# Attention and mixture of experts on one core: the order of work in the expert stage, the loads of its records and the copies of its hidden layer changed

## The chip, the cores and the metric

One core of one Trainium2 chip runs the whole program. The metric is the device time of one execution in microseconds. Everything is computed in 32-bit floating point. TensorE multiplies matrices and writes to PSUM, VectorE and ScalarE do elementwise work and read PSUM back, GpSimd adds and scales rows and issues the indirect DMAs, and SyncE issues the plain DMAs.

## The reference, cut to what matters

```python
x = conv_attention(x)                    # local attention, 2 images of 32 x 32 tokens, 128 channels
t = tokens(x)                            # 2048 tokens of 128
t = t + additive_attention(norm(t))      # h = tanh(q_i + k_j + bh), e = h @ Wa
h = norm(t)
logits = h @ gate_w + gate_b             # 8 experts
idx = argmax(softmax(logits)); prb = max(softmax(logits))
pos = place of the token among those of its expert      # kept if pos < 320
hmid = relu(buf @ w1 + b1)               # buf: 8 experts x 320 slots x 128, w1: 128 x 512
y = (hmid @ w2 + b2) * prb               # w2: 512 x 128
t = t + nan_to_num(y, nan=0, posinf=1e4, neginf=-1e4)
```

## The kernel before

The work stands in one program for each engine, written out by hand; the engines meet at semaphores only, and each engine does its instructions in the order of its program. There are three stages: local attention, additive attention over 16 blocks of 128 query tokens (`p` counts them), and the experts. The change concerns the passage from the second to the third, and the third.

**From attention to records.** For each block p, `soften_main(p)` (ScalarE) takes the exponential of the energies, `turn_main(p)` (TensorE) transposes it in two halves of four blocks, `turned_main(p)` (VectorE) copies the halves to SBUF, `attend(p, half)` (TensorE) multiplies each with the tokens, and `attended(p)` and `normed(p)` (VectorE) make the record's contents. Then `turn_normed`, `logits` (TensorE) and `route(p)` (VectorE) pick the expert, `counts(p)` (TensorE) counts the tokens of each expert so far, `slotted(p)` (VectorE) turns that into the row of the record, and `scatter(p)` (GpSimd) writes the 128 records of the block to `xbuf` in DRAM. Of the last two blocks, the steps of p = 14 that follow `attend` are written among those of p = 15, behind the last energies.

A record is a row of 272 numbers: the normed token (C = 128), the token itself (128), the logits less their maximum (8) and the token's number, with 7 unused. `xbuf` has 2560 such rows, 20 tiles of 128. Experts take 320 rows each, so two experts share five tiles: `tiles_of(e)` gives an even expert the first two and an odd one the last three, the middle tile of the five being half of one and half of the other.

**Experts.** SyncE loads `xbuf` back in four DMAs of five tiles (`xe`, semaphores `ld_xe[q]`). TensorE turns five tiles at a time (`turn_slots(q)`) into banks 4 and 5, ScalarE copies them to `xeT` (`turned_slots`), `first_product(e)` multiplies with w1 into banks 0 to 3 (four matmuls of 320 columns, each shown as two instructions), `rectified(e)` adds the bias, takes the maximum with 0 and writes `h`: ScalarE for two of the four banks, VectorE for the other two. `second_product(e)` multiplies with w2 into slots of banks 6 and 7 (`slot_bank`), three parts for each expert, of 128, 128 and 64 rows. TensorE's order is: first product of e + 1, then second product of e.

VectorE ends the work in `slots_out(e)`: for each tile the product times `prb` plus the weighted bias row `b2w`, then over the two or three tiles of the expert together six operations that replace infinities and NaNs and add the token (`high`, `low`, `good`, `fill`, `fill`, `ye`). A helper `Chain` (`link`) puts a semaphore wait behind every operation. `weights(q)` (exponential on ScalarE, sum and reciprocal on VectorE) gives `prb` for five tiles. VectorE does it in the turn of expert 2q - 2 and says so with `prb_ready`. GpSimd scales the 20 bias rows and after that sends the 20 tiles to `out`:

```python
for q in range(NE // 2):
    pool.wait_ge(prb_ready, q + 1)
    for k in range(q * n, (q + 1) * n):
        last = nc.gpsimd.tensor_scalar(b2w[:, k, :], b2w[:, k, :], prb[:, k:k + 1], 1.0, ALU.mult, ALU.mult)
    last.then_inc(b2w_ready, 1)
```

Each send is an indirect DMA of 128 rows of 512 B, to the rows named by `dest`. The program ends when all have landed.

## Time and profile before

| | |
|---|---|
| median of 3 runs | 765.26 us (763.8 to 765.88) |
| the profiled execution | 758.97 us |
| its span in the trace | 757.2 us |
| busy: TensorE, VectorE, ScalarE, GpSimd | 532.6, 565.6, 579.9, 418.0 us |
| first issue of the loads of the records | at 687.79 us of the span |
| TensorE's last matmul ends | at 740.28 us |

The span runs from the first to the last event of the trace, and the execution's time lies 1.8 us above it. Busy time is an average over stages with different limits: the stage of the experts, from 692 us on, is a small part of it and has to be read by itself. An idle engine is shown with what ended its idle time.

### The profile page before, as it was taken

Reading aid. Unit: us, or ns where it says so; the run is one execution under the profiler, and the core shown is the slowest. Engines: PE = TensorE matmul, PEld = TensorE weight load, DVE = VectorE, ACT = ScalarE, POOL = GpSimd, SP = SyncE. Lnnn points to the kernel's source line nnn. Section 1 sums busy time; section 2 is a strip of 40 time slices with the busy share of each in tenths; the row PEclk is TensorE's granted clock in tenths of the full one; section 3 lists DMA queues with packets and bytes.
Section 4 is the critical chain, followed back from the end, with each engine's and each line's share of the span. In section 5 each row is a group of like instructions: output and inputs, shape, how many; then the busy total and the mean of one; then the engine's idle time right before and its main releaser. Section 6 shows DMA issues by size and latency. Waiting matters only on the chain.

```text
span 757.2 us, 11927 instructions
## 1 busy us (share of the span) xinstructions
PE 532.6 (70%) x4440; PEld 261.0 (34%) x4440; DVE 565.6 (75%) x1326; ACT 579.9 (77%) x385; POOL 418.0 (55%) x453
## 2 busy tenths in 40 slices
PE   7899998886357676675775786766666666744991
PEld 3666665662012131221221231221221221233870
DVE  3566688877986878878878788878878878741783
ACT  2367776655379999999999999999999999911210
POOL 2000000005448888888878878878878878601156
PEclk9899999998689999999999999999999999985996
DMA  9500000007000000000000000000000000004001
GB/s 324 164 3 1 2 2 2 2 1 292 0 1 0 5 12 1 12 8 4 12 1 12 12 0 13 12 1 13 12 0 12 12 1 12 10 6 149 2 11 39
DMA packets 11225, 22.22 MB, mean 29 GB/s; under 512 B 1232, under 2 KB 8434, under 8 KB 10400
## 3 DMA queue, kind: packets, MB, share of 16 engines
q1 hardware_dynamic: 9760, 18.56, 6.9%
q0 software_dynamic: 1408, 2.91, 1.1%
q8 instruction: 35, 0.57, 0.3%
q14 instruction: 22, 0.18, 0.1%
HBM read 14.73 MB, written 7.37 MB: 29 GB/s over the span
## 4 chain that ended last, share of the span: by engine, by line
issue 34%; ACT 30%; PE 16%; DVE 12%; POOL 2%; DMA 1%; POOLq 0%; DVEq 0%; ACTq 0%; SPq 0%
ACT arena L788 28%; PE ps L461 3%; PE ps L474 2%; PE ps L443 2%; POOL out L406 2%; DVE arena L1020 2%; DVE arena L871 2%; ACT pm L792 1%; PE ps L500 1%; PE ps L695 1%; PE ps L587 1%; PE ps L492 1%; PE ps L708 1%; PE ps L484 1%; DVE mean L918 1%
## 5 line engine op out<-in xcount | busy, mean ns | idle before, releaser
L370 POOL TENSOR_SCALAR arena<-k,q 128x1024 f32<-128x1024 f32 (+1 forms) x384 | 370.3, 981 | 268.9 <-DVE q L998 172.1
L788 ACT ACTIVATE arena<-arena 128x4096 f32<-128x4096 f32 x128 | 451.3, 3614 | 23.8 <-DVE arena L1020 23.8
L587 PE MATMUL ps<-arena,cst 128*32 128x512 f32 x2048 | 255.4, 619 | 166.7 <-ACT arena L788 162.1
L1020 DVE TENSOR_SCALAR arena<-ps,q 128x512 f32<-128x512 f32 (+1 forms) x256 | 248.2, 1012 | 64.0 <-PE ps L587 58.3
L587 PEld LDWEIGHTS ps<-arena,cst 128*32 128x32 f32 x2048 | 55.5, 112 | 322.9 <-ACT arena L788 233.2
L743 ACT ACTIVATE arena<-arena,mn 128x320 f32<-128x320 f32 (+1 forms) x128 | 62.7, 539 | 33.7 <-DVE mn L871 32.5
L871 DVE CUSTOM_DVE_ANT_0 arena<-ps,arena 128x320 f32<-128x320 f32 (+1 forms) x128 | 53.0, 470 | 17.0 <-PE ps L443 12.0
L461 PE MATMUL ps<-cst,arena 128*128 128x128 f32 x352 | 56.4, 293 | 3.4 <-ACT arena L750 3.4
L461 PEld LDWEIGHTS ps<-cst,arena 128*128 128x128 f32 x352 | 41.9, 151 | 13.4 <-ACT arena L750 6.3
L750 ACT ACTIVATE arena<-ps 128x512 f32<-128x512 f32 x56 | 32.9, 588 | 11.1 <-PE ps L461 11.1
L610 PE MATMUL ps<-x_one,ptm 128*128 128x129 f32 x256 | 37.9, 293 | 2.0 <-DVE ptm L1036 2.0
L610 PEld LDWEIGHTS ps<-x_one,ptm 128*128 128x128 f32 x256 | 32.3, 199 | 15.5 <-issue 12.6
L378 POOL DMA_INDIRECT xbuf<-rec,slots x16 | 16.1, 1007 | 26.5 <-DVEq L119 24.4
L804 ACT ACTIVATE arena<-ps 128x512 f32<-128x512 f32 x4 | 2.4, 597 | 34.5 <-PE ps L683 34.5
L880 DVE COPY arena<-ps 128x512 f32<-128x512 f32 x32 | 22.0, 689 | 8.6 <-PE ps L461 8.6
L474 PE MATMUL ps<-arena 128*32 128x128 f32 x704 | 26.9, 285 | 1.1
L398 POOL TENSOR_SCALAR arena<-arena,prb 128x128 f32<-128x128 f32 x20 | 7.0, 370 | 34.0 <-DVEq L119 34.0
L1027 DVE CUSTOM_DVE_ANT_0 pm<-ps,cst 128x1024 f32<-128x1024 f32 x16 | 19.6, 1223 | 7.3 <-PE ps L587 5.9
L708 PE MATMUL ps<-arena 128*128 128x128 f32 (+1 forms) x192 | 24.1, 279 | 0.7 <-issue 0.7
L406 POOL DMA_INDIRECT out<-ye,dest x20 | 20.4, 1020 | 5.9 <-issue 5.9
L708 PEld LDWEIGHTS ps<-arena 128*128 128x128 f32 (+1 forms) x192 | 22.0, 174 | 4.0 <-issue 1.6
L474 PEld LDWEIGHTS ps<-arena 128*32 128x32 f32 x704 | 18.3, 113 | 11.6 <-issue 6.9
(134 smaller groups left out, 559.0 us busy)
## 6 DMA issues: line engine op xcount, KB each, us to landing
arena<-in_w SPq DMA_DIRECT2D x2, 2048.0 KB, 10.2
xbuf<-rec SPq DMA_DIRECT2D x1, 2720.0 KB, 13.9
arena<-xbuf SPq DMA_DIRECT2D x4, 680.0 KB, 6.3
arena<-in_inner SPq DMA_DIRECT2D x1, 1280.0 KB, 10.6
arena<-in_b SPq DMA_DIRECT2D x1, 1280.0 KB, 15.0
tokens<-in_xT SPq DMA_DIRECT2D x4, 256.0 KB, 5.8
arena<-in_top SPq DMA_DIRECT2D x1, 1024.0 KB, 6.7
arena<-in_bottom SPq DMA_DIRECT2D x1, 1024.0 KB, 14.8
```

Source lines behind the costliest of these rows:

```text
L370: last = nc.gpsimd.tensor_scalar(ring[t % 3][:, c, 0:n], k4[:, img * L:img * L + n], q4[:, m:m + 1], 1.0, ALU.add, ALU.mult)
L406: nc.gpsimd.indirect_dma_start(out_d, bass.IndirectOffsetOnAxis(ap=dest[:, k:k + 1], axis=0), ye[:, k, :], None, bounds_check=NT - 1, oob_ ...
L461: last = nc.tensor.transpose(bank(to, g * P, (g + 1) * P), prob[r][:, g, c * P:(c + 1) * P], c_("ident"))
L474: last = nc.tensor.matmul(bank(6, r * P, (r + 1) * P)[g * HP:(g + 1) * HP, :], vals[:, value_block(j, c), 2 * g + r, :], pts[r][:, c, g * ...
L587: last = nc.tensor.matmul(bank(half)[c * U:(c + 1) * U, :], c_("wa", U - QPG - QPG * s, 2 * U - QPG - QPG * s), ring[t % 3][:, c, half * 5 ...
L610: last = nc.tensor.matmul(bank(6, 0, C + 1), ptm[:, k, :], x_one[:, p // BPI * BPI + k, :], start=(k == 0), stop=(k == BPI - 1))
L708: last = nc.tensor.matmul(to[row:row + n, :], h[e % 2][:, c, at:at + n], w2[:, e, c, :], start=(c == 0), stop=(c == FC - 1))
L743: nc.scalar.activation(prob[r][:, g, 0:n], nlog[r][:, g, 0:n], ACT.Exp, bias=mn[r][:, g:g + 1], scale=-1.0).then_inc(p_ready, 1)
L750: nc.scalar.activation(pts[rho % 2][:, c, :], bank(turn_bank(rho, c)), ACT.Copy).then_inc(pta_ready, 1)
L788: nc.scalar.activation(ring[t % 3], ring[t % 3], ACT.Tanh).then_inc(h_ready, 1)
L871: nc.vector.tensor_tensor_reduce(out=nlog[r][:, g, 0:n], in0=bank(g, 0, n), in1=btab[kind][:, 2 * g + r, :], scale=-1.0, scalar=3e38, op0= ...
L1020: last = nc.vector.tensor_scalar(ring[t % 3][:, c, lo:L], keys[:, lo:L], q4[:, m:m + 1], None, ALU.add)
```

## The change

Eight edits, all behind the last energies of the second stage:

- VectorE does `turned_main(15)` before `slotted(14)`, and TensorE does `attend(15, 0)` before `counts(14)`.
- The load of the records is cut otherwise: first the 128 numbers of the normed token for tiles 0 to 2, then the same for tiles 3 and 4, then everything else of all 20 rows (`xr`, 144 numbers a row), then the normed tokens of tiles 5 to 19.
- `turn_slots` fills bank 4 with three tiles and bank 5 with two, and `first_product(e)` waits for e + 1 copies, so an even expert needs only the first copy of its five tiles.
- ScalarE does all four rectifying copies of every expert.
- The weights of all 20 tiles are computed in one piece.
- GpSimd scales ten bias rows, sends two tiles, scales five, sends five, scales five and sends the rest.
- The semaphores `w2_done`, `ye_ready` and `y_out` count tiles, not experts; some links of the chain are left out. Tiles 18 and 19 get banks 4 and 5.
- Expert 7's three tiles go through VectorE one by one, each sent when it is done.

TensorE's program from the first `turn_normed(14)` of the end to the first record's slot reads so before (L619 is `turn_normed`, L625 `logits`, L601 `turn_main`, L632 and L633 `counts`, L610 `attend`):

```order
L619 MATMUL ps<-cst,rec0 128x128
L625 MATMUL ps<-cst,xnT 128x8
L601 MATMUL ps<-cst,pm 128x128 x8
L632 MATMUL ps<-oh,cst 128x8
L633 MATMUL ps<-osum,ones 128x8
L610 MATMUL ps<-x_one,ptm 128x129 x8
L619 MATMUL ps<-cst,rec1 128x128
```

and so after it (L633, L639, L615, L646 and L647, L624 in the same order of names):

```order
L633 MATMUL ps<-cst,rec0 128x128
L639 MATMUL ps<-cst,xnT 128x8
L615 MATMUL ps<-cst,pm 128x128 x8
L624 MATMUL ps<-x_one,ptm 128x129 x4
L646 MATMUL ps<-oh,cst 128x8
L647 MATMUL ps<-osum,ones 128x8
L624 MATMUL ps<-x_one,ptm 128x129 x4
L633 MATMUL ps<-cst,rec1 128x128
```

The first half of block 15's product now stands ahead of block 14's counts. VectorE's program at the same place, before (the last row of `route(14)`, then `slotted(14)`, then the two copies of `turned_main(15)`; L119 is the end of a chain):

```order
L1079 TENSOR_SCALAR rec0<-lg,mx 128x8
L119 ISA
L1087 TENSOR_TENSOR over<-ps,cst 128x8
L1088 SCALAR_TENSOR_TENSOR over<-over,ps 128x8
...
L1092 TENSOR_SCALAR slots0<-slot 128x1
L119 ISA
L1036 COPY ptm<-ps 128x512 x2
L1047 RECIPROCAL rzm<-ps 128x1
```

and after:

```order
L1085 TENSOR_SCALAR rec0<-lg,mx 128x8
L119 ISA
L1042 COPY ptm<-ps 128x512 x2
L1093 TENSOR_TENSOR over<-ps,cst 128x8
L1094 SCALAR_TENSOR_TENSOR over<-over,ps 128x8
...
L1098 TENSOR_SCALAR slots0<-slot 128x1
L119 ISA
L1053 RECIPROCAL rzm<-ps 128x1
```

The two copies have moved ahead of `slotted(14)`. GpSimd's program from the last scatters of records to its end, before (L398 scales a bias row, L406 sends a tile):

```order
L378 DMA xbuf<-rec1,slots1 2560x272
L398 TENSOR_SCALAR arena<-arena,prb 128x128 x20
L406 DMA out<-ye,dest 2048x128 x20
```

and after:

```order
L386 DMA xbuf<-rec1,slots1 2560x272
L404 TENSOR_SCALAR arena<-arena,prb 128x128 x10
L409 DMA out<-ye,dest 2048x128 x2
L404 TENSOR_SCALAR arena<-arena,prb 128x128 x5
L409 DMA out<-ye,dest 2048x128 x5
L404 TENSOR_SCALAR arena<-arena,prb 128x128 x5
L409 DMA out<-ye,dest 2048x128 x13
```

The first sends now stand behind ten scalings, not twenty. The diff, cut to its core (what is left out are semaphore names):

```diff
-        xe = arena[:, o:o + TILES * REC].rearrange("p (n c) -> p n c", n=TILES)
-        o += TILES * REC
+        xe = arena[:, o:o + TILES * C].rearrange("p (n c) -> p n c", n=TILES)
+        o += TILES * C
+        xr = arena[:, o:o + TILES * (REC - C)].rearrange("p (n c) -> p n c", n=TILES)
+        o += TILES * (REC - C)
...
         def slot_bank(k):
 
+            if k >= TILES - 2:
+                return bank(k - TILES + 6, 0, P)
             k %= 5
             return bank(6, k * P, (k + 1) * P) if k < 2 else bank(7, (k - 2) * P, (k - 1) * P)
...
-            for q in range(NE // 2):
-                n = TILES // (NE // 2)
-                src = xbuf_d[q * n * P:(q + 1) * n * P, :].rearrange("(n p) c -> p n c", p=P)
-                sp.dma_start(xe[:, q * n:(q + 1) * n, :], src).then_inc(ld_xe[q], 16)
+            def fetch(to, lo, hi, c0, c1, done):
+                src = xbuf_d[lo * P:hi * P, c0:c1].rearrange("(n p) c -> p n c", p=P)
+                sp.dma_start(to[:, lo:hi, :], src).then_inc(done, 16)
+
+            fetch(xe, 0, 3, 0, C, ld_xe[0])
+            fetch(xe, 3, 5, 0, C, ld_xe[1])
+            fetch(xr, 0, TILES, C, REC, ld_xr)
+            fetch(xe, 5, TILES, 0, C, ld_xe[2])
...
-            n = TILES // (NE // 2)
-            pool.wait_ge(ld_b2, 16)
-            for q in range(NE // 2):
-                pool.wait_ge(prb_ready, q + 1)
-                for k in range(q * n, (q + 1) * n):
+            def weighted_bias(q):
+                pool.wait_ge(prb_ready, 1)
+                for k in range(5 * q, 5 * q + 5):
                     last = nc.gpsimd.tensor_scalar(b2w[:, k, :], b2w[:, k, :], prb[:, k:k + 1], 1.0, ALU.mult, ALU.mult)
                 last.then_inc(b2w_ready, 1)
+
+            def send(k):
+                pool.wait_ge(y_out, k + 1)
+                nc.gpsimd.indirect_dma_start(out_d, bass.IndirectOffsetOnAxis(ap=dest[:, k:k + 1], axis=0),
+                                             ye[:, k, :], None, bounds_check=NT - 1,
+                                             oob_is_err=False).then_inc(out_st, 16)
+
+            pool.wait_ge(ld_b2, 16)
+            weighted_bias(0)
+            weighted_bias(1)
             pool.wait_ge(dest_ready, 1)
             for i in range(2):
                 pool.wait_ge(t2_st[i], 16 * NB // 2)
-            for e in range(NE):
-                pool.wait_ge(y_out, e + 1)
-                for k in tiles_of(e):
-                    nc.gpsimd.indirect_dma_start(out_d, bass.IndirectOffsetOnAxis(ap=dest[:, k:k + 1], axis=0),
-                                                 ye[:, k, :], None, bounds_check=NT - 1,
-                                                 oob_is_err=False).then_inc(out_st, 16)
+            for k in range(TILES):
+                if k in (2, 7):
+                    weighted_bias(2 + k // 5)
+                send(k)
...
             turn_main(p)
+            attend(p, 0)
             counts(p - 1)
-            attend(p, 0)
             attend(p, 1)
...
-                pe.wait_ge(ld_xe[q], 16)
                 if q:
+                    pe.wait_ge(ld_xe[2], 16)
                     pe.wait_ge(xeT_ready, 2 * q)
                 for k in range(5):
-                    last = nc.tensor.transpose(bank(4 + k // 4, k % 4 * P, (k % 4 + 1) * P), xe[:, 5 * q + k, 0:C],
+                    if q == 0 and k in (0, 3):
+                        pe.wait_ge(ld_xe[k // 3], 16)
+                    last = nc.tensor.transpose(bank(4 + k // 3, k % 3 * P, (k % 3 + 1) * P), xe[:, 5 * q + k, :],
                                                c_("ident"))
-                    if k >= 3:
+                    if k in (2, 4):
                         last.then_inc(xeT_done, 1)
 
             def first_product(e):
-                pe.wait_ge(xeT_ready, 2 * (e // 2) + 2)
+                pe.wait_ge(xeT_ready, e + 1)
                 for c in range(FC):
-                    if e and c < 2:
-                        pe.wait_ge(ha_ready, 2 * e - 1 + c)
-                    elif e:
-                        pe.wait_ge(hd_ready, 2 * e - 3 + c)
+                    if e:
+                        pe.wait_ge(h_out, FC * (e - 1) + c + 1)
                     nc.tensor.matmul(bank(c, 0, CAP), w1[:, e, c * P:(c + 1) * P], xeT[:, e * CAP:(e + 1) * CAP],
                                      start=True, stop=True).then_inc(w1_done, 1)
 
             def second_product(e):
-                pe.wait_ge(ha_ready, 2 * e + 2)
-                pe.wait_ge(hd_ready, 2 * e + 2)
-                if e >= 2:
-                    pe.wait_ge(ye_ready, e - 1)
+                pe.wait_ge(h_out, FC * (e + 1))
                 for k, row, at, n in parts_of(e):
                     to = slot_bank(k)
-                    if e % 2 == 0 and e and n == HALF:
-                        pe.wait_ge(ye_ready, e)
+                    if k >= 5:
+                        pe.wait_ge(ye_ready, k // 5 * 5 - 3 if k % 5 < 2 else k // 5 * 5)
                     for c in range(FC):
                         last = nc.tensor.matmul(to[row:row + n, :], h[e % 2][:, c, at:at + n], w2[:, e, c, :],
                                                 start=(c == 0), stop=(c == FC - 1))
-                last.then_inc(w2_done, 1)
+                    if row + n == P:
+                        last.then_inc(w2_done, 1)
...
+                for i in range(2):
+                    act.wait_ge(xeT_done, 2 * q + i + 1)
+                    n, at = (3 - i) * P, (5 * q + 3 * i) * P
+                    nc.scalar.activation(xeT[:, at:at + n], bank(4 + i, 0, n), ACT.Copy).then_inc(xeT_ready, 1)
 
             def rectified(e):
                 if e >= 2:
-                    act.wait_ge(w2_done, e - 1)
-                for c in range(2):
+                    act.wait_ge(w2_done, (e - 2) // 2 * 5 + (2 if e % 2 == 0 else 5))
+                for c in range(FC):
                     act.wait_ge(w1_done, FC * e + c + 1)
                     nc.scalar.activation(h[e % 2][:, c, :], bank(c, 0, CAP), ACT.Relu,
-                                         bias=c_("b1", e * FC + c, e * FC + c + 1)).then_inc(ha_ready, 1)
+                                         bias=c_("b1", e * FC + c, e * FC + c + 1)).then_inc(h_out, 1)
 
             turned_slots(0)
-            weights(0)
             rectified(0)
+            act.wait_ge(ld_xr, 16)
+            nc.scalar.activation(lge[:, :, :], xr[:, :, C:C + NE], ACT.Exp).then_inc(ge_ready, 1)
...
+            turned_main(p)
             slotted(p - 1)
-            turned_main(p)
             attended(p)
...
+            dve.wait_ge(ld_xr, 16)
+            nc.vector.tensor_copy(dest[:, :], xr[:, :, C + NE]).then_inc(dest_ready, 1)
+            dve.wait_ge(ge_ready, 1)
+            link(nc.vector.tensor_reduce(zg[:, :], lge[:, :, :], AX, ALU.add))
+            nc.vector.reciprocal(prb[:, :], zg[:, :]).then_inc(prb_ready, 1)
+            link.end()
 
             def slots_out(e):
 
-                dve.wait_ge(w2_done, e + 1)
+                tiles = tiles_of(e)
                 dve.wait_ge(b2w_ready, e // 2 + 1)
-                tiles = tiles_of(e)
-                n = len(tiles)
-                y = ye[:, tiles[0]:tiles[0] + n, :]
-                for k in tiles:
-                    link(nc.vector.scalar_tensor_tensor(ye[:, k, :], slot_bank(k), prb[:, k:k + 1], b2w[:, k, :],
-                                                        ALU.mult, ALU.add))
-                dve.sem_inc(ye_ready, 1)
-                link(nc.vector.tensor_scalar(high[:, 0:n, :], y, FLT_MAX, 1e4, ALU.is_gt, ALU.mult))
-                link(nc.vector.tensor_scalar(low[:, 0:n, :], y, -FLT_MAX, -1e4, ALU.is_lt, ALU.mult))
-                link(nc.vector.tensor_scalar(good[:, 0:n, :], y, 0.0, 0.0, ALU.mult, ALU.is_equal))
-                link(nc.vector.tensor_tensor(fill[:, 0:n, :], high[:, 0:n, :], low[:, 0:n, :], ALU.add))
-                link(nc.vector.copy_predicated(fill[:, 0:n, :], good[:, 0:n, :], y))
-                link(nc.vector.tensor_tensor(y, fill[:, 0:n, :], xe[:, tiles[0]:tiles[0] + n, C:2 * C], ALU.add))
-                link.end()
-                dve.sem_inc(y_out, 1)
-
-            weights(0)
-            rectified(0)
+                if e == 0:
+                    dve.wait_ge(prb_ready, 1)
+                groups = [(k,) for k in tiles] if e == NE - 1 else [tiles]
+                for group in groups:
+                    for k in group:
+                        dve.wait_ge(w2_done, group[-1] + 1)
+                        nc.vector.scalar_tensor_tensor(ye[:, k, :], slot_bank(k), prb[:, k:k + 1], b2w[:, k, :],
+                                                       ALU.mult, ALU.add).then_inc(ye_ready, 1)
+                    n = len(group)
+                    y = ye[:, group[0]:group[0] + n, :]
+                    dve.wait_ge(ye_ready, group[-1] + 1)
+                    nc.vector.tensor_scalar(high[:, 0:n, :], y, FLT_MAX, 1e4, ALU.is_gt, ALU.mult)
+                    link(nc.vector.tensor_scalar(low[:, 0:n, :], y, -FLT_MAX, -1e4, ALU.is_lt, ALU.mult))
+                    nc.vector.tensor_scalar(good[:, 0:n, :], y, 0.0, 0.0, ALU.mult, ALU.is_equal)
+                    link(nc.vector.tensor_tensor(fill[:, 0:n, :], high[:, 0:n, :], low[:, 0:n, :], ALU.add))
+                    link(nc.vector.copy_predicated(fill[:, 0:n, :], good[:, 0:n, :], y))
+                    nc.vector.tensor_tensor(y, fill[:, 0:n, :], xr[:, group[0]:group[0] + n, 0:C],
+                                            ALU.add).then_inc(y_out, n)
+                    link.end()
```

## Rows read from the trace of the kernel before

**Rows 1.** The page, busy time, share of the span and instructions of each engine.

```profile
PE 532.6 (70%) x4440; PEld 261.0 (34%) x4440; DVE 565.6 (75%) x1326; ACT 579.9 (77%) x385; POOL 418.0 (55%) x453
```

**Rows 2.** Chain of waits, 680 to 757 us: start, length, what.

```profile
684.87 0.71 issue
...
687.79 4.13 DMA arena<-xbuf
...
752.94 0.97 POOL out L406
```

**Rows 3.** Windows: length, busy (instructions) by engine, clock, DMA share, GB/s.

```profile
672.00:676.00 4.00, 3.40 (x16) 3.21 (x16) 1.14 (x2) 0.00 (x0) 0.97 (x1) 0.57 0.04 11
...
694.00:698.00 4.00, 4.00 (x8) 2.63 (x9) 0.33 (x3) 1.12 (x3) 0.00 (x0) 0.50 0.80 266
698.00:700.00 2.00, 2.00 (x10) 1.54 (x9) 1.15 (x3) 0.49 (x1) 1.59 (x5) 0.67 0.02 4
700.00:736.00 36.00, 36.00 (x230) 29.41 (x229) 27.27 (x69) 8.70 (x23) 11.89 (x23) 1.00 0.01 3
```

**Rows 4.** Groups by line and form, 685 us to the end, GpSimd and ScalarE.

```profile
L406 POOL DMA_INDIRECT out<-ye,dest x20 | 20.4, 1020 | 5.9 <-issue 5.9
L398 POOL TENSOR_SCALAR arena<-arena,prb 128x128 f32<-128x128 f32 x20 | 7.0, 370 | 34.0 <-DVEq L119 34.0
...
L818 ACT ACTIVATE arena<-ps,cst 128x320 f32<-128x320 f32 x16 | 7.9, 529 | 18.5 <-PE ps L695 18.5
```

**Rows 5.** Timeline, TensorE and VectorE, 669 to 677 us: start, length, instruction.

```profile
669.16 1.10 PE L601 MATMUL ps<-cst,pm 128*128 128x128 f32 x8 [0.59 <-ACT pm L792]
669.66 0.23 DVE L1079 TENSOR_SCALAR rec<-lg,mx 128x8 f32<-128x8 f32 x1
671.85 1.29 DVE L1036 COPY ptm<-ps 128x512 f32<-128x512 f32 x2 [0.25 <-DVE slots L1092]
672.60 3.40 PE L610 MATMUL ps<-x_one,ptm 128*128 128x129 f32 x16 [2.00 <-DVE ptm L1036]
676.04 0.17 DVE L1047 RECIPROCAL rzm<-ps 128x1 f32<-128x1 f32 x1 [2.90 <-PE ps L610]
```

**Rows 6.** Timeline, 692 to 699 us.

```profile
692.06 1.30 PE L683 MATMUL ps<-cst,arena 128*128 128x128 f32 x5 [8.35 <-DMA arena<-xbuf]
693.18 0.60 ACT L804 ACTIVATE arena<-ps 128x512 f32<-128x512 f32 x1 [24.08 <-PE ps L683]
...
694.00 4.64 PE L695 MATMUL ps<-arena 128*128 128x320 f32 x8 [0.64 <-ACT arena L806]
...
697.64 0.18 DVE L1149 CAST dest<-arena 128x20 uint32<-128x20 f32 x1 [12.93 <-DMA arena<-xbuf]
...
698.43 1.16 PE L683 MATMUL ps<-cst,arena 128*128 128x128 f32 x5
```

**Rows 7.** DMA queues, 687 to 698.5 us: packets, MB, share of 16 engines.

```profile
q1 hardware_dynamic: 2624, 2.79, 72.7%
```

**Rows 8.** DMA queues, 659 to 662 us, with one store of 64 KB.

```profile
q1 hardware_dynamic: 144, 0.07, 7.7%
```

**Rows 9.** Timeline, VectorE and TensorE, 736 us to the end.

```profile
736.13 1.01 DVE L1161 TENSOR_SCALAR arena<-ps,cst 128x320 f32<-128x320 f32 x2 [0.25 <-DVE ye L1180]
...
737.24 3.04 PE L708 MATMUL ps<-arena 128*64 128x128 f32 x24 [0.68 <-issue]
737.93 0.29 DVE L1175 TENSOR_SCALAR high<-ye 128x256 f32<-128x256 f32 x1
...
739.86 0.42 DVE L1180 TENSOR_TENSOR ye<-fill,arena 128x256 f32<-128x256 f32 x1
740.53 1.12 DVE L1172 SCALAR_TENSOR_TENSOR ye<-ps,prb,arena 128x128 f32<-128x128 f32 x3 [0.25 <-DVE ye L1180]
741.80 0.36 DVE L1175 TENSOR_SCALAR high<-ye 128x384 f32<-128x384 f32 x1
...
744.20 0.56 DVE L1180 TENSOR_TENSOR ye<-fill,arena 128x384 f32<-128x384 f32 x1
```

37 lines of the change are left out of this document (2 added, 35 removed).

## The prediction

> **What bounds the kernel now.** I read the page's busy shares first: no engine is full over the whole span, VectorE and ScalarE are busy three quarters of it [rows 1]. So the stages have to be read apart, and the edit touches only the last 90 us. There I followed the chain of waits, then the stretches in windows, then single rows of the timeline.
>
> Three stretches bound the end in turn. From 669 to 686 us one serial chain runs through TensorE and VectorE for the last two blocks' records [rows 2, 5]. From 694 to 740.3 us TensorE sets the pace: it is busy for 36.00 of the 36 us from 700 to 736 [rows 3]. From then on it has nothing to do and GpSimd alone is left: 20 scatters, 1.02 us each and 0.30 us (5.9 over 20) between two of them [rows 4]. The last begins at 752.94 [rows 2], so the first began near 752.94 - 19 x 1.32 = 727.9. They are late because the last scaling of bias rows stands ahead of all of them in GpSimd's order, and it waits for the last `prb_ready`, which VectorE gives only in expert 4's turn. TensorE's end at 740.28 is thus followed by 16.92 us of tail. The profiled execution took 758.97 us, the median of the runs shown is 765.26; I make the sum against the first and subtract it from the second.
>
> **The swap ahead of the experts.** Now VectorE ends `route(14)` at 669.89, does `slotted(14)`, and only at 671.85 begins `turned_main(15)`; TensorE starts `attend(15)` at 672.60 and VectorE takes its result at 676.04 [rows 5]. After it, `turned_main(15)` starts when `route(14)` has been closed, near 670.1 (TensorE's first four turned blocks are there by 669.16 + 0.55), and the first copy, 1.29 / 2 = 0.65 us, lets TensorE start near 670.85, 1.75 earlier. Its 16 matmuls took 3.40 us at a granted clock of 0.57 on average, that is almost all at the lower level [rows 3, 5]. The matmuls of `counts(14)`, of 8 columns, will stand between the halves. With `slotted(14)` they fill the 1.6 us from 670.26, where the turned blocks end, to 671.85; I give them 0.5 and `slotted(14)` 1.1. All at the lower level the end is 670.85 + 3.9 = 674.75; with the first half at the full clock 0.85 less. `slotted(14)` lies beside the second half of `attend(15)` (1.7 us). The gain is 1.3 to 2.1; I take **1.7**. Everything below is in the times of before, without this shift. Scatter 14 leaves GpSimd later than before but still long before scatter 15.
>
> **Loads of the records.** Now TensorE starts 4.13 us after the first of four issues, on the first 680 KB [rows 2]; all four have landed at 697.64 [rows 6]. The first fetch is now 384 pieces of 512 B instead of 640 of 1088 B. The bytes of a first fetch fall from 680 to 192 KB. How a short read starts up is in no row; it is bounded from both sides by the streaming of 2.79 MB in 0.727 x 11.5 = 8.4 us [rows 7]: by bytes, the 0.50 MB less are 1.5 us, by pieces, the 256 less are 256 x 51 / 16 ns = 0.8. I take 1.1: TensorE starts at 690.95. It needs tiles 3 and 4 too (another 128 KB, 0.4 us on), and the first copy of ScalarE is of 384 columns after three turned tiles: 0.83 + 0.5 + 0.1 us where it was 1.12 + 0.60 + 0.22 [rows 6]. `first_product(0)` then begins at about 692.4, not 694.00. But what follows it, `turn_slots(1)`, waited for nothing at 698.43 and now waits for the very last fetch. A piece of 1088 B takes 0.727 x 16 x 11.5 / 2624 = 51 ns of one engine, with a few small ones [rows 7]; one of 512 B, in the store of 64 KB, 0.077 x 16 x 3 / 144 = 26 ns [rows 8]. 2560 pieces of 512 and 2560 of 576 B (29 ns by their bytes) are 141 us over 16 engines against 131: 0.6 us more, all landed at 698.2. TensorE would be ready at 692.4 + 4.4 = 696.8 and stands until 698.2. So of 1.6 us **0.25** is left. The bounds: nothing more to land (697.6, gain 0.8), or each piece at the price of a 1088 B one (8.2 us more, a loss of 7.9).
>
> In a sentence of its own: the Trainium skill, DMA: Bandwidth & Descriptors, Rules for kernel authors, advises at least 1 MiB per DMA and to coalesce, and speaks against cutting this load in other and smaller pieces; it gives no price for 512 B at which the sum could be redone.
>
> **ScalarE does all rectifying copies.** 32 instead of 16 in this stage, 0.53 us each [rows 4]: 17 us over 46, four (2.1 us) inside the 5.5 us of an expert (698.43 to 740.28 over seven and a half); TensorE's next use of them is behind a second product of 3 us. That costs nothing. If that cover were gone, each expert would wait up to 0.5 us. VectorE loses 16 copies (two took 1.01), off the path except at one place: `second_product(7)` stood 0.68 us because VectorE came to expert 7's copies only at 736.13 [rows 9]. That goes: **0.68**. TensorE's end is 740.28 - 0.25 - 0.68 = 739.35, called T.
>
> The weights in one piece (ScalarE's exponential behind `rectified(0)`, near 697.5; GpSimd's two scalings of five rows, 5 x 0.37 = 1.85 us each, until about 702 [rows 4]) are ready before expert 0's second product ends near 704. Waits on `ye_ready` for each tile fall on tiles read a product earlier. The two later scalings lie between sends 1 and 2, and 6 and 7, while GpSimd needs 0.7 + 2.5 x 1.3 = 4.0 us of each 5.5: nothing.
>
> **The end.** From `high` to the last addition VectorE takes 2.35 us for two tiles (737.93 to 740.28) and 2.96 for three (741.80 to 744.76) [rows 9], so 0.61 a tile and 1.74 for one; with the scaled sum (1.12 / 3 = 0.37) and the steps between (0.15 and 0.25 now, less with fewer links) a tile's turn is 1.9 to 2.5 us; I take 2.15. Expert 6's two tiles are ready when two of the three parts of its second product are done (a third of 3 us each), T - 3.04 - 1.0; its group takes 3.0, so VectorE is free at T - 0.9, and tiles 17, 18, 19 are out at T + 1.1, + 3.3 and + 5.4. As one group they would be out at T + 4.25 or so; the pieces buy only the two sends that would follow. GpSimd, by then idle, needs 0.7 us from the signal (as at 684.87) to the start of the scatter, and from there to the end of the span 757.2 - 752.94 = 4.26 [rows 2]. The end is T + 10.4 where it was 16.92: **6.5**.
>
> Sum: 1.7 + 0.25 + 0.68 + 6.5 = 9.1 us. Span 748.1, the profiled execution 749.9, the median 765.26 - 9.1 = **756.1 us**. For scale, 0.3% (2.3 us) is about what a measurement of this kernel tells from no change.
>
> **Rivals.**
> Small pieces load slowly. For it: no row shows a read of 512 B rows out of 1088; against: the store's 26 ns. Halfway to the upper bound the last fetch lands 3.8 us later than I forecast, TensorE stands that much more: 9.1 - 3.8 = 5.3, 760.0 us. 11%.
>
> The clock returns late. TensorE's granted clock was 0.50 until about 699.3 (0.67 over 698 to 700), 5.3 us after its work became unbroken at 694.0 [rows 3]. If the new stand until 698.2 restarts that, it returns at 703.5 and 4.2 us run at half speed: 2.1 lost, 758.2 us. The other way, an earlier return, gives up to 0.6. 12%. The rule behind it is the Trainium skill's, TensorE: Matmul & The Clock Gate, on oscillation: waits for DMA between bursts of matmuls bring the lower level back.
>
> The swap brings nothing, because `counts` between the halves delays the end of `attend` as much as the early start saves: 7.4 gained, 757.9 us. 5%.
>
> The change does not do what it says: GpSimd stays behind, since a send that waits costs 0.7 more. Were that so for every tile, 2.0 us a tile against TensorE's 5.5 / 2.5 = 2.2, it would still keep up; the sends would have to take twice 1.02. Then the tail keeps its 16.9 and 2.6 remain, 762.7 us. 2%.
>
> Slower than before: the same load, but where a piece costs as much as a large one and more. The gain is gone when the last fetch lands 9.1 us later than forecast, 9.1 x 16 / 5120 = 28 ns more on each piece, 56 ns; at 65 ns it is 9.1 - 11.7, 767.9 us. Only above 56 does it decide, and the rows have 26. 3%.
>
> The forecast itself 67%, with a range of its own from 753.8 to 758.0. Beyond all these something faster has little room. The whole range, 753.2 to 760.0, leaves out the last two rivals and the upper part of the first. Faster 0.94, within 0.3% 0.03, slower 0.03.
>
> **What would show it.** In the changed profile: the swap, if `attend(15)`'s result is taken near 674.3; the load, if `turn_slots(1)` waits for a DMA and all has landed 10.4 us after the first issue; ScalarE, if TensorE has no gap before expert 7's second product; the end, if GpSimd's last scatter begins 6.1 us after TensorE's last matmul and waits for VectorE. The prediction is wrong if that distance is near 12 us, or if the stand before `turn_slots(1)` is over 3 us.

## The result, and the profile after

| | before | after |
|---|---|---|
| median of 4 runs each, one chip | 765.57 us (763.80 to 766.09) | 751.95 us (751.35 to 752.69) |
| ratio, with its 95% interval | | 0.9827 [0.9807, 0.9847] |
| profiled execution, its span | 758.97 us, 757.2 | 752.69 us, 750.9 |

By the ratio the change gives 13.2 us where 9.1 was forecast, and the median lies below the range. The two profiled executions differ by 6.3 us only, and the runs below say where these two differences part. Some comparisons below had single executions in a slower state (831.86 and 2747.0 us of the kernel before beside runs 13 to 16, 1705.84 beside runs 9 and 10), which no ratio counts.

**The swap and the load.** Timeline of the kernel after, TensorE, VectorE, ScalarE and SyncE's queue, 669 to 703 us (start, length, instruction):

```profile
669.58 1.10 PE L615 MATMUL ps<-cst,pm 128*128 128x128 f32 x8 [0.59 <-ACT pm L804]
...
671.02 1.16 PE L624 MATMUL ps<-x_one,ptm 128*128 128x129 f32 x8 [0.34 <-DVE ptm L1042]
672.02 0.29 PE L646 MATMUL ps<-oh,cst 128*128 128x8 f32 x2
...
672.39 1.14 PE L624 MATMUL ps<-x_one,ptm 128*128 128x129 f32 x8
...
673.81 0.17 DVE L1053 RECIPROCAL rzm<-ps 128x1 f32<-128x1 f32 x1 [0.28 <-DVE slots L1098]
...
685.55 4.98 SPq L334 DMA_DIRECT2D arena<-xbuf  x4
...
688.14 1.30 PE L699 MATMUL ps<-cst,arena 128*128 128x128 f32 x5 [6.65 <-DMA arena<-xbuf]
689.59 4.06 PE L709 MATMUL ps<-arena 128*128 128x320 f32 x8 [0.15 <-ACT arena L817]
...
697.23 1.33 PE L699 MATMUL ps<-cst,arena 128*128 128x128 f32 x5 [3.58 <-DMA arena<-xbuf]
698.35 4.47 PE L709 MATMUL ps<-arena 128*128 128x320 f32 x8
```

`counts(14)` stands between the halves of `attend(15)`, as forecast. From the first turned probabilities to the result it takes 673.81 - 669.58 = 4.23 us; it was 676.04 - 669.16 = 6.88 [rows 5]. The swap gives 2.65 us here. The load begins TensorE 2.6 us after the first issue (4.1 before [rows 2]), but `turn_slots(1)` waits 3.58 us for the last fetch, until 11.7 us after the first issue. A stand of over 3 us there was named in the prediction as a sign that it is wrong. Windows of the kernel after (length, busy us and instructions of TensorE, its weight loads, VectorE, ScalarE, GpSimd, then granted clock, DMA share, GB/s):

```profile
672.00:676.00 4.00, 1.52 (x14) 1.33 (x12) 2.56 (x14) 0.00 (x0) 0.97 (x1) 0.98 0.06 20
693.65:697.20 3.55, 0.01 (x1) 0.00 (x0) 0.78 (x3) 0.78 (x3) 1.92 (x6) 0.88 0.80 198
697.20:700.00 2.80, 2.77 (x9) 2.18 (x10) 0.00 (x0) 1.15 (x3) 1.58 (x5) 0.50 0.00 0
700.00:703.00 3.00, 3.00 (x8) 2.02 (x7) 0.00 (x0) 1.38 (x4) 0.00 (x0) 0.50 0.00 0
703.00:706.00 3.00, 3.00 (x25) 2.71 (x24) 0.97 (x4) 0.39 (x1) 0.00 (x0) 0.97 0.02 5
```

From 672 to 676 us the clock is at the upper of its two levels (1.2 and 2.4 GHz), where it was 0.57 on average [rows 3]; that is why `attend(15)` is shorter than forecast. In the 3.55 us in which TensorE stands it is granted at 0.88, and from the moment that it works again it is at the lower level for 5.8 us: `first_product(1)` takes 4.47 us, while the expert products behind it take 2.3.

**The end.** Timeline of the kernel after, from 733 us:

```profile
734.91 5.44 PE L719 MATMUL ps<-arena 128*128 128x128 f32 x48
...
737.60 0.97 POOL L409 DMA_INDIRECT out<-ye,dest  x1 [3.38 <-DVE ye L1176]
738.88 0.99 POOL L409 DMA_INDIRECT out<-ye,dest  x1 [0.30 <-issue]
...
739.95 0.34 DVE L1166 SCALAR_TENSOR_TENSOR ye<-ps,prb,arena 128x128 f32<-128x128 f32 x1
...
745.22 0.29 DVE L1176 TENSOR_TENSOR ye<-fill,arena 128x128 f32<-128x128 f32 x1
...
746.66 0.97 POOL L409 DMA_INDIRECT out<-ye,dest  x1 [0.30 <-issue]
```

Experts 6 and 7's second products run without a gap to 740.35; the tail behind is 750.9 - 740.35 = 10.55 us (forecast 10.4, before 16.92). The last scatter begins 6.31 us after TensorE's end (forecast 6.1) and, against the forecast, doesn't wait for VectorE: eight scatters stand back to back from expert 5's tiles on.

### The profile page after: what moved, and what is told of

It is laid out like the page before. It is cut to its first block, busy times and chain, and to the rows that moved or that the text cites. A ratio compares the mean times of both kernels' runs of the same rounds, so it can differ in the third digit from the quotient of the medians.

```text
span 750.9 us, 11918 instructions
## 1 busy us (share of the span) xinstructions
PE 533.7 (71%) x4440; PEld 260.3 (35%) x4440; DVE 556.6 (74%) x1316; ACT 588.4 (78%) x398; POOL 418.5 (56%) x453
## 4 chain that ended last, share of the span: by engine, by line
issue 33%; ACT 29%; PE 17%; DVE 13%; DMA 2%; POOL 1%; POOLq 0%; DVEq 0%; SPq 0%; ACTq 0%
ACT arena L800 28%; PE ps L475 3%; PE ps L488 2%; PE ps L457 2%; PE ps L719 2%; PE ps L709 2%; DVE arena L1026 2%; DVE arena L877 2%; ACT pm L804 1%; PE ps L514 1%; DMA arena<-xbuf 1%; PE ps L506 1%; PE ps L498 1%; DVE mean L924 1%; DVE sv L931 1%
## 5 line engine op out<-in xcount | busy, mean ns | idle before, releaser
L601 PE MATMUL ps<-arena,cst 128*32 128x512 f32 x2048 | 255.8, 620 | 166.4 <-ACT arena L800 161.8
L601 PEld LDWEIGHTS ps<-arena,cst 128*32 128x32 f32 x2048 | 55.3, 111 | 323.2 <-ACT arena L800 232.8
L877 DVE CUSTOM_DVE_ANT_0 arena<-ps,arena 128x320 f32<-128x320 f32 (+1 forms) x128 | 53.1, 471 | 16.9 <-PE ps L457 11.9
L475 PEld LDWEIGHTS ps<-cst,arena 128*128 128x128 f32 x352 | 41.7, 150 | 13.5 <-ACT arena L762 6.3
L762 ACT ACTIVATE arena<-ps 128x512 f32<-128x512 f32 x56 | 33.0, 589 | 10.9 <-PE ps L475 10.9
L624 PE MATMUL ps<-x_one,ptm 128*128 128x129 f32 x256 | 36.8, 286 | 0.3 <-DVE ptm L1042 0.3
L624 PEld LDWEIGHTS ps<-x_one,ptm 128*128 128x128 f32 x256 | 31.1, 191 | 14.0 <-issue 12.6
L824 ACT ACTIVATE arena<-ps,cst 128x320 f32<-128x320 f32 x32 | 16.3, 530 | 16.7 <-PE ps L709 16.5
L817 ACT ACTIVATE arena<-ps 128x384 f32<-128x384 f32 (+1 forms) x8 | 3.2, 436 | 29.9 <-PE ps L699 29.9
L709 PE MATMUL ps<-arena 128*128 128x320 f32 x64 | 22.8, 506 | 0.2 <-ACT arena L817 0.2
```

The source lines that it names most:

```text
L475: last = nc.tensor.transpose(bank(to, g * P, (g + 1) * P), prob[r][:, g, c * P:(c + 1) * P], c_("ident"))
L601: last = nc.tensor.matmul(bank(half)[c * U:(c + 1) * U, :], c_("wa", U - QPG - QPG * s, 2 * U - QPG - QPG * s), ring[t % 3][:, c, half * 5 ...
L624: last = nc.tensor.matmul(bank(6, 0, C + 1), ptm[:, k, :], x_one[:, p // BPI * BPI + k, :], start=(k == 0), stop=(k == BPI - 1))
L709: nc.tensor.matmul(bank(c, 0, CAP), w1[:, e, c * P:(c + 1) * P], xeT[:, e * CAP:(e + 1) * CAP], start=True, stop=True).then_inc(w1_done, 1)
L762: nc.scalar.activation(pts[rho % 2][:, c, :], bank(turn_bank(rho, c)), ACT.Copy).then_inc(pta_ready, 1)
L877: nc.vector.tensor_tensor_reduce(out=nlog[r][:, g, 0:n], in0=bank(g, 0, n), in1=btab[kind][:, 2 * g + r, :], scale=-1.0, scalar=3e38, op0= ...
```

## The experiments

Each was timed beside the kernel before on its chip, in five rounds. Unless said otherwise an edit is to the changed kernel.

**1. The kernel before, again, unaltered.** 

> The kernel before, unchanged. Its profiled execution took 759.0 us, while four others took 763.8 to 766.1; the changed kernel's profiled execution and three others all lie between 751.3 and 752.7. Theory A: the 6.6 us between the profiled execution of before and the others is lost behind 740 us, in the end of the kernel that the change rewrites; then a profile of a slow-end execution shows a tail longer than 16.9 us after TensorE's last matmul, or a TensorE stretch between 692 and 740 us with more of it at the lower clock. Theory B: it is lost ahead of 640 us, in stages that both kernels share, and the gain of 13.6 us is in part chance; then the expert stage again takes 65 us from TensorE's first transpose to the end of the span, and the extra 6 us is seen before.

765.13 us (763.55 to 766.17, 12 runs), ratio 1.0004 [0.9993, 1.0014], profiled at 763.9 with a span of 762.1. So here is a profile of an execution of the usual length, 4.9 us longer than the one the prediction was made from. Its timeline, from 735 us:

```profile
735.53 3.04 PE L708 MATMUL ps<-arena 128*64 128x128 f32 x24 [0.68 <-issue]
...
737.47 0.74 DVE L1172 SCALAR_TENSOR_TENSOR ye<-ps,prb,arena 128x128 f32<-128x128 f32 x2 [2.04 <-remote]
...
747.01 0.97 POOL L406 DMA_INDIRECT out<-ye,dest  x1 [0.30 <-issue]
750.21 1.12 DVE L1172 SCALAR_TENSOR_TENSOR ye<-ps,prb,arena 128x128 f32<-128x128 f32 x3 [9.46 <-remote]
...
755.32 0.97 POOL L406 DMA_INDIRECT out<-ye,dest  x1 [7.33 <-DVEq L119]
756.59 0.97 POOL L406 DMA_INDIRECT out<-ye,dest  x1 [0.30 <-issue]
757.87 0.97 POOL L406 DMA_INDIRECT out<-ye,dest  x1 [0.30 <-issue]
```

TensorE's last matmul ends, as modelled, at 738.57. VectorE waits for its signal until 750.21, with a releaser that the profile can't name ("remote"; only one core runs). In the profile of before it began at 740.53, 0.25 us after TensorE [rows 9]. GpSimd meanwhile sends 17 scatters back to back from 726.02 to 747.98, then stands 7.33 us for expert 7's tiles. The tail is 762.1 - 738.57 = 23.5 us, not 16.9.

**2. Without the swap** (both lines as in the kernel before).

```diff
             turn_main(p)
+            counts(p - 1)
             attend(p, 0)
-            counts(p - 1)
             attend(p, 1)
...
+            slotted(p - 1)
             turned_main(p)
-            slotted(p - 1)
```

> The changed kernel with the order of attend and counts on TensorE and of turned_main and slotted on VectorE at block 15 put back. Theory A, each step of the sum stands by itself: 2.2 us slower than the changed kernel (the trace of the changed kernel shows SyncE's first load at 685.55 instead of 687.79), 754.2 us, ratio to before 0.985. Theory B, the swap's gain is only that attend(15) ran at the full clock by chance of phase: 1.0 us or less, 753.0 us or less.

755.77 us, 0.9881 [0.9864, 0.9898]; by the ratios the swap is worth (0.9881 - 0.9827) x 765 = 4.1 us, with an error of 2.0. Above the forecast of both theories; `attend(15)` takes 3.81 us here in one piece, at a granted clock of 0.50 (672 to 674 us).

**3. The load split in five fetches**: tiles 5 to 9 come ahead of the rest of the records.

```diff
             fetch(xe, 3, 5, 0, C, ld_xe[1])
+            fetch(xe, 5, 10, 0, C, ld_xe[2])
             fetch(xr, 0, TILES, C, REC, ld_xr)
-            fetch(xe, 5, TILES, 0, C, ld_xe[2])
+            fetch(xe, 10, TILES, 0, C, ld_xe[3])
...
-                    pe.wait_ge(ld_xe[2], 16)
+                    pe.wait_ge(ld_xe[2 if q == 1 else 3], 16)
```

> The changed kernel with the normed tokens of tiles 5 to 9 in a fetch of their own ahead of the rest of the records, so that turn_slots(1) does not wait for the last fetch. Theory A, TensorE stands 3.6 us there because everything must land first and the lower clock lasts longer for it: turn_slots(1) begins right behind first_product(0), 3.5 us earlier, and the end is 3 to 5 us earlier, 747 to 749 us. Theory B, the end is bound by GpSimd's sends from expert 5 on, whatever TensorE does, or the later clock return is chance: 0 to 1.5 us earlier, 750.5 to 752 us.

745.75 us, 0.9747 [0.9730, 0.9764]: 6.1 us faster than the changed kernel by the ratios (error 2.0). Its timeline, TensorE, and under it a window:

```profile
688.96 3.96 PE L710 MATMUL ps<-arena 128*128 128x320 f32 x8 [0.15 <-ACT arena L818]
692.76 0.71 PE L700 MATMUL ps<-cst,arena 128*128 128x128 f32 x5
693.31 2.32 PE L710 MATMUL ps<-arena 128*128 128x320 f32 x8
```

```profile
693.00:697.00 4.00, 4.00 (x27) 3.37 (x26) 0.78 (x3) 3.15 (x8) 1.54 (x5) 1.00 0.74 188
```

No wait before `turn_slots(1)`, and the full clock stays from 693 on: the wait and the slow 5.8 us behind it go together. The tail is longer than in the changed kernel, 744.4 - 732.92 = 11.5 us against 10.55 (more on this at run 9).

**4. The kernel before, with only GpSimd's scalings put between its scatters.**

```diff
-            for q in range(NE // 2):
+            def weighted_bias(q):
...
+            weighted_bias(0)
+            weighted_bias(1)
...
             for e in range(NE):
+                if e in (2, 4):
+                    weighted_bias(e // 2 + 1)
                 pool.wait_ge(y_out, e + 1)
```

> The kernel before with one edit: GpSimd scales the bias rows of experts 4 and 5 and of 6 and 7 between the sends instead of ahead of all of them. Theory A, the end was bound by GpSimd's 20 sends that began at 727.7: the last send begins after VectorE's last group at 744.8 + 0.7 + 2 x 1.3 = 748.1 instead of 752.9, 4.8 us less, 760.5 us against 765.3 (ratio 0.9937). Theory B, the executions of before at 765 us lose another 6 us in the same place (GpSimd's late scalings), and interleaving removes that too: 10 to 11 us less, 755 us. Rival: the sends between the scalings delay the scalings, VectorE waits for b2w_ready and TensorE for VectorE: no gain.

752.64 us, 0.9837 [0.9818, 0.9857], 12.5 us less than before: nearly the whole change, and more than both theories had. Its timeline:

```profile
735.51 3.04 PE L714 MATMUL ps<-arena 128*64 128x128 f32 x24 [0.68 <-issue]
...
738.83 1.12 DVE L1178 SCALAR_TENSOR_TENSOR ye<-ps,prb,arena 128x128 f32<-128x128 f32 x3 [0.25 <-issue]
```

VectorE begins expert 7 at 738.83, 0.28 us after TensorE's 738.55.

**5. The same, and the swap.** 

> The kernel before with two of the change's parts: GpSimd's scalings between its scatters, and the swap ahead of the experts. Theory A (parts add; the swap gave 3.8 us when it was taken out of the changed kernel; the scatters alone gave 752.6 us): about 749 us, which would leave the new loads and ScalarE's rectifying copies together at a loss of 3 us in the changed kernel at 751.9. Theory B (the swap is worth only the 1.7 us of the prediction, the rest of the 3.8 came from how it meets the new loads): about 751 us.

749.75 us, 0.9803 [0.9790, 0.9816]: the swap gives 2.6 us (error 1.8).

**6. Whole records**: the load of the kernel before in the changed kernel.

```diff
-            fetch(xe, 0, 3, 0, C, ld_xe[0])
-            ...
+            for q in range(4):
+                src = xbuf_d[q * 5 * P:(q + 1) * 5 * P, :].rearrange("(n p) c -> p n c", p=P)
+                sp.dma_start(xe[:, q * 5:(q + 1) * 5, :], src).then_inc(ld_xe[q], 16)
...
+                pe.wait_ge(ld_xe[q], 16)
...
```

> The changed kernel, but the records are loaded as in the kernel before, in four fetches of five tiles of whole rows of 1088 bytes; transposes of tiles 0 to 4 wait for the first of them, the weights and VectorE's addresses for all four. Theory A (the changed order of loads costs: 3.6 us of wait before turn_slots(1) and a clock that falls behind it): 2 to 5 us faster than the changed kernel, 747 to 750 us, with no wait for a DMA at turn_slots(1) and the full clock from about 699. Theory B (the first fetch of 680 KB starts TensorE 1.5 us later, and the rest is a wash): within 1 us of the changed kernel.

747.19 us, 0.9769 [0.9754, 0.9784]. The new order of loads costs 4.4 us (error 1.9). `turn_slots(1)` waits for no DMA. All four fetches are there at 694.25, 9.9 us after the first issue at 684.33, and not 11.7.

**7. A backlog**: all four scalings first, and GpSimd held until ten tiles are ready.

```diff
-            weighted_bias(0)
-            weighted_bias(1)
+            for q in range(4):
+                weighted_bias(q)
...
+            pool.wait_ge(y_out, 10)
             for k in range(TILES):
-                if k in (2, 7):
-                    weighted_bias(2 + k // 5)
                 send(k)
```

> The changed kernel with all four scalings ahead of the scatters, and GpSimd held back until ten tiles are ready, so that its 20 scatters run back to back from about 728 us as in the kernel before. Theory A (a long unbroken run of GpSimd scatters holds back the signal of TensorE's last product until about 1 us after the run ends): the modelled end of TensorE's work stays near 740.4, the signal comes only near 751, VectorE's last group is late, the last scatter begins near 757 and the kernel takes 762 to 764 us. Theory B (the late signal of the kernel before has nothing to do with the scatters): signal at 740.4, last scatter at 727.9 + 19 x 1.28 = 752.3, 757 to 758.5 us.

761.30 us, 0.9947 [0.9934, 0.9961]. Its timeline, TensorE, and under it the first row of its waits from 730 us (us in total, times, longest):

```profile
733.46 2.97 PE L718 MATMUL ps<-arena 128*128 128x128 f32 x24
736.70 1.90 PE L718 MATMUL ps<-arena 128*64 128x128 f32 x10 [0.27 <-ACT arena L823]
738.92 0.27 PE L718 MATMUL ps<-arena 128*128 128x128 f32 x1 [0.32 <-issue]
...
743.88 1.07 PE L718 MATMUL ps<-arena 128*128 128x128 f32 x4 [1.47 <-issue]
745.98 0.58 PE L718 MATMUL ps<-arena 128*128 128x128 f32 x2 [1.03 <-issue]
```

```profile
DVE ye L1165 <- remote: 10.5, 1, 10.5
```

Here the starts of the matmuls themselves are torn apart: from 736.7 on TensorE comes on in pieces until 746.6, with gaps up to 1.47 us in which it waits for nothing that the profile shows. The signals are late before that. The first product of expert 7 ends, as modelled, at 733.62, and ScalarE gets its last part only at 736.12, with a wait of 1.22 us on "remote". Theory A had only the signal late, and later (751); the last scatter begins at 755.28 instead of 757, and the time lies 0.7 us below its range. It is still 3 us above theory B's, and VectorE's long wait is there.

**8. The kernel before, GpSimd held until TensorE is done.**

```diff
+            pool.wait_ge(w2_done, NE)
             for e in range(NE):
```

> The kernel before, with GpSimd waiting for TensorE's last product before its first scatter. Theory A (the scatters hold TensorE's signal back): with no scatter under way VectorE begins expert 7's tiles right at TensorE's end, near 740.5, and is done near 744.8; the 20 scatters run from about 741.3 to 766, span about 770, 771 to 773 us in all. Theory B (the signal is late by itself, near 750): the scatters begin near 751, the last at 775, 781 us in all.

771.55 us, 1.0089 [1.0074, 1.0105], as theory A has it. Timeline:

```profile
736.28 3.04 PE L709 MATMUL ps<-arena 128*64 128x128 f32 x24 [0.68 <-issue]
...
739.58 1.12 DVE L1173 SCALAR_TENSOR_TENSOR ye<-ps,prb,arena 128x128 f32<-128x128 f32 x3 [0.25 <-DVE ye L1181]
```

With no scatter under way TensorE's signal is there at once, on the same chip as run 7.

**9. The backlog, broken three times**: after 5, 10 and 15 scatters five rows are scaled that nobody reads any more.

```diff
+            pool.wait_ge(b2w_ready, 4)
             for k in range(TILES):
+                if k in (5, 10, 15):
+                    for r in range(k - 5, k):
+                        nc.gpsimd.tensor_scalar(b2w[:, r, :], b2w[:, r, :], prb[:, r:r + 1], 1.0, ALU.mult, ALU.mult)
                 send(k)
```

> The kernel of the run with the backlog, whose run of scatters is now broken three times, after 5, 10 and 15 of them: GpSimd scales five rows again (1.8 us) that nobody reads any more; the values sent are unchanged. Theory A (what holds TensorE back is a run of scatters without another instruction of some length between them): TensorE's signal and VectorE's last groups are late by no more than the rest of a run of five, the last scatter begins at 725.4 + 19 x 1.28 + 3 x 1.9 = 755.4 by GpSimd's own work, 761 to 762 us. Theory B (it is the backlog, whatever lies between): TensorE's matmuls stand as long as before or longer, the signal near 750, the last scatter near 759 or later, 764 us or more. The time alone is a weak test; the start of VectorE's tiles of expert 7 decides, 740 to 743 for A, 749 or later for B.

761.30 us, 0.9948 [0.9936, 0.9960] (the kernel before 765.66): the time of run 7, by GpSimd's own work now (its last scatter begins at 754.68). At expert 7 TensorE is whole again and VectorE at once behind it:

```profile
727.50 3.07 PE L722 MATMUL ps<-arena 128*64 128x128 f32 x24
...
731.89 0.87 DVE L1169 SCALAR_TENSOR_TENSOR ye<-ps,prb,arena 128x128 f32<-128x128 f32 x3 [4.77 <-PE ps L722]
...
732.56 5.44 PE L722 MATMUL ps<-arena 128*128 128x128 f32 x48
...
738.51 0.34 DVE L1169 SCALAR_TENSOR_TENSOR ye<-ps,prb,arena 128x128 f32<-128x128 f32 x1
```

But a run of five is felt too. The product of expert 5 ends, as modelled, at 730.57, and VectorE gets it at 731.89, 1.3 us later and 1.1 us after the end of the fifth scatter (730.79); ScalarE's first copy of expert 7 begins with it, at 731.92. Run 3, with five scatters there too, has the same two starts at 726.75 and 726.78, 1.3 us after a product that ended at 725.49. That its tail is 0.9 us longer than the changed kernel's fits this, but was not tested. Run 6 has five scatters as well (until 727.66). There VectorE gets the product 0.1 us after its end, at 727.63, and ScalarE's first copy of expert 7 is 0.5 us late: it begins 1.28 us after that product (728.64 against 727.36), and 0.80 us after it in run 14.

**10. The kernel of run 3 with expert 7 in one group** (`groups = [tiles]`). 

> The version with the load split in five fetches (745.75 us), with expert 7's three tiles in one group on VectorE instead of one by one. Theory A (sending the last tiles one by one buys almost nothing, since GpSimd has a backlog of eight scatters from expert 5 on and is the last anyway): VectorE out at TensorE's end + 4.3, the last scatter at + 7.6 instead of + 7.3, 746 us. Theory B (the tiles one by one save what they look like, two scatters of 1.28 us each): 748.3 us.

745.88 us, 0.9743 [0.9730, 0.9756]. Tile by tile buys nothing measurable in that kernel, because GpSimd is the last by its backlog: all eight scatters from expert 5's tiles on stand back to back in one group too.

**11. The kernel of run 3 with VectorE doing half the rectifying copies** (chunks 2 and 3, ahead of the tiles of the expert before). 

> The version with the load split in five fetches (745.75 us), with VectorE again doing the rectifying copies of chunks 2 and 3 of every expert, ahead of the tiles of the expert before. Theory A (the term of the prediction: TensorE stands 0.68 us before expert 7's second product, because VectorE comes late, and GpSimd's backlog passes about that on): 746.4 us. Theory B (VectorE has room, and ScalarE's four copies a round cost TensorE as much as they save): 745.5 to 745.9. Theory C (VectorE's two copies come late in every expert, since its tile work for three tiles takes 3.9 us ahead of them): 748 us or more.

746.68 us, 0.9756 [0.9739, 0.9772]; by the ratios 0.7 us over run 3, with an error of 1.8. In its trace TensorE stands 0.80 us before expert 7's second product, as theory A has it; the times alone don't tell it from nothing.

**12. The backlog with two short breaks** (as 9, after 5 and 10, one row each). 

> The kernel of the run with the broken backlog, with two breaks instead of three, after 5 and 10 scatters, and each only one scaling of one row (0.37 us) that nobody reads any more. By GpSimd's own work the last scatter begins at 724.6 + 19 x 1.28 + 2 x 0.5 = 750. Theory A (any other instruction between the scatters lets TensorE through): VectorE begins expert 7's tiles near 738.5, as with the long breaks, and the kernel takes 756 to 757.5 us, since nothing is late. Theory B (it is the pause that counts, 1.8 us of it, and 0.4 is too short): TensorE stands as in the unbroken backlog, VectorE begins them near 749, 761 to 763 us.

756.68 us, but the kernel before took 758.58 us (757.36 to 759.26, 15 runs) on this chip: 0.9982 [0.9973, 0.9991]. The question of run 12 is not answered, and another is put: the stall isn't on every chip. In the rest four kernels, and then two, ran side by side on a chip each.

**13 to 16. The changed kernel, and the backlog unbroken, broken and with short breaks.**

> The changed kernel unaltered, beside the next three on one chip. The last run was on a chip on which the kernel before took 758.6 us and not 765 as on the five before it. If this chip is of the first kind, before 765 and this 752 us; if it is of the second, before 758.6 and this 750 to 752, since this kernel has no long run of scatters that could be felt.

> The kernel of the first run with the backlog (unbroken run of 20 scatters) again. Theory A (the run of scatters holds TensorE back, on chips of the first kind alone): 761 us where before takes 765, with VectorE's first tile of expert 7 near 749; and where before takes 758.6, 755.5 us, that tile near 738. Theory B (it is not the chip but chance from one call to the next): the two kernels don't change together, 761 us beside before at 758.6, or 755.5 beside 765.

> The backlog with three breaks of five scalings each. Theory A: on a chip of either kind the last scatter begins near 755 by GpSimd's own work and VectorE begins expert 7's tiles near 738.5, 761 us. Theory B (the single profile of it was a lucky one): VectorE's tiles near 749 on a chip of the first kind, 763 us or more.

> The backlog with two breaks of one scaling each (0.37 us). On a chip of the first kind: Theory A (any other instruction between the scatters lets TensorE through) 756.7 us, VectorE's tiles of expert 7 from 738.5; Theory B (0.4 us is too short a break) 761 us or more, those tiles near 749. On a chip of the second kind it is 756.7 us by both.

This chip again gave the kernel before 758.42 us. The changed kernel 751.57, 0.9905 [0.9890, 0.9919]; the unbroken backlog 755.62, 0.9963 [0.9951, 0.9976]; broken 762.08, 1.0047 [1.0034, 1.0060]; with short breaks 757.58, 0.9994 [0.9983, 1.0005]. The unbroken backlog, timeline:

```profile
725.85 1.05 POOL L409 DMA_INDIRECT out<-ye,dest  x1 [24.50 <-issue]
...
733.89 5.44 PE L718 MATMUL ps<-arena 128*128 128x128 f32 x48
...
738.75 0.34 DVE L1165 SCALAR_TENSOR_TENSOR ye<-ps,prb,arena 128x128 f32<-128x128 f32 x1
...
750.57 0.97 POOL L409 DMA_INDIRECT out<-ye,dest  x1 [0.30 <-issue]
```

The same program as run 7, the same 20 scatters in one run, and no stall. The broken backlog is the program of run 9, and here expert 5's product, which ends at 732.31, reaches VectorE in 0.1 us:

```profile
729.24 3.07 PE L722 MATMUL ps<-arena 128*64 128x128 f32 x24
...
732.41 0.87 DVE L1169 SCALAR_TENSOR_TENSOR ye<-ps,prb,arena 128x128 f32<-128x128 f32 x3 [3.55 <-PE ps L722]
```

So the 1.3 us of run 9 are the same thing in small.

**17 and 18. Short breaks and the unbroken backlog, a third time.** 

> The backlog with two breaks of one scaling each, once more, hoping for a chip of the kind on which the kernel before takes 765 us. There: Theory A (any other instruction between the scatters lets TensorE through) 756.7 us, VectorE's tiles of expert 7 from 738.5; Theory B (0.4 us is too short a break) 761 us or more, those tiles near 749. Where before takes 758.5 us it tells nothing new: 757 us.

> The unbroken backlog beside it: 761 us with VectorE's first tile of expert 7 near 749 where before takes 765, 755.6 us and that tile near 738.5 where before takes 758.5.

Before 758.21 us; 757.73, 0.9988 [0.9977, 1.0000], and 755.53, 0.9971 [0.9956, 0.9985]. Again a chip without the stall, so whether 0.4 us is enough of a break stays open.

## Why the prediction was wrong

**The step that failed** is the sum's frame: "I make the sum against the first and subtract it from the second". It takes the profiled execution for one like those that make the median. The profiled execution of before (758.97 us) has no stall, the median (765.26) has one, and they lie 6.3 us apart when the runs shown agree within 2.1. In the first comparison and on the four chips of runs 1 to 11 the kernel before took 764.9 to 765.7 us; on the three other chips of runs 12 to 18 it took 758.2 to 758.6, just what the profile showed. The changed kernel takes 752 on either sort (751.95 and 751.57). So the gain is 13.2 us (0.9827) where the stall is and 7.2 us (0.9905) where it isn't; the difference of 6 us is what the stall costs the kernel before. Against the execution that it was made from, the sum of 9.1 was thus too large, not too small. That the profiled execution came from a chip of the second sort fits, but is argued only: its chip isn't known, and on the chip of runs 5 to 8 one execution of the kernel before took 760.82 us among others of 763.85 to 765.7, so one that mostly escapes the stall isn't excluded. Nor are chip and hour told apart: each chip was used for one set of runs, and all sets with the stall came before all sets without it.

**The term that was mis-sized by it** is "The end", 6.5 us. Against the typical execution of run 1 the tail falls from 23.5 to 10.55 us, by 13.0; against the profiled one it falls by 6.4. The tail after came out right, 10.55 against 10.4, in part by luck: it was to be bound by VectorE's last tile, and GpSimd's backlog ended at nearly the same time. GpSimd's order alone gives 12.5 us (run 4). That a long run of scatters is what stalls TensorE is shown on chips of the first sort in three ways: adding it (run 7) brings the stall, taking it away (runs 4 and 8) removes it, and breaking it (run 9) leaves 1.3 us of it at one place. How it reaches TensorE is not shown. None of the rivals spoke of this; a rival "the profiled execution isn't the typical one" should have had a chance.

**The swap** was right in mechanism and too small: 1.7 forecast (1.3 to 2.1); 2.65 in the trace, 2.6 and 4.1 us in the pairs (errors 1.8 and 2.0). The granted clock stayed at 0.98, where TensorE stands only 0.34 us ahead of `attend(15)` and not 2.00 us [rows 5]; in run 2, with that stand, the same work is at 0.50 and takes 3.81 us.

**Loads of the records**: the sign was wrong. Forecast +0.25; all landed at 11.7 us after the first issue, not 10.4. TensorE stood 3.58 us where 1.4 was forecast: 1.3 for the later landing, and 0.9 because it was ready earlier, 8.1 us after the first issue and not 9.0. And the rival "The clock returns late", priced at 2.1 us, came on top: `first_product(1)` alone took 2.15 us more. Together 4.4 us lost (error 1.9) against run 6. The price of a piece: 0.747 x 13.5 x 16 = 161 us for 5184 pieces, from this view of the queues, 685 to 698.5 us:

```profile
q1 hardware_dynamic: 5184, 2.79, 74.7%
```

That is 31 ns each, where I had 27.5. Few ns, but 5120 of them over 16 engines: 1.1 us.

On the clock behind such a stand the Trainium skill, TensorE: Matmul & The Clock Gate, on oscillation, was the better guide, and the trace agrees (clock 0.50 from 697.2 to 703 after a stand of 3.58 us).

**ScalarE's copies**: forecast 0.68; the gap is gone after, and back as 0.80 us in run 11. Right by the trace, and too small for the times.

**The last tiles one by one**: I had them buy two sends. VectorE's turn per tile, 1.83 us, is shorter than my 2.15, and GpSimd had eight scatters queued, so it wasn't waiting. In run 3's kernel they buy nothing (run 10). For the changed kernel an estimate is 0.9 us: in run 10 the group is out 3.96 us after TensorE's end, 0.7 to the next scatter and 2 x 1.28 more put the last one at 7.2, where it began at 6.31.

The parts in a chain, each against the one before by ratio: GpSimd's order -12.5, the swap -2.6, ScalarE's copies with the weights in one piece, the tiles one by one and the links left out -2.6 (0.9803 to 0.9769), the loads +4.4, in sum -13.2 before rounding. The last -2.6 (error 1.5) is more than the terms that I gave it. The traces of runs 5 and 6 have 1.9 of it in the tail, 12.3 us in run 5 and 10.45 in run 6: in run 5 GpSimd stands 2.25 us for VectorE's group of expert 7, which takes 4.39 us, where the same group with fewer links takes 3.66 in run 10. How much of that the links give is not tested by itself. In the profiled pair the forecast span was 748.1, found 750.9, 2.8 more: the loads' 1.3, the clock's 2.1 and a stage that began 0.42 later, less 0.95 of the swap, are 2.9.
